# A gated recurrence of 256 steps on one core: steps written out, gate biases brought in by ScalarE, and the split state packed

## The reference

```python
ys = cond / 16
d = rsqrt(einsum('bi,io->bo', ys * ys, W * W) + 1e-8)
x = x + einsum('bsi,io->bso', x * ys[:, None, :], W) * d[:, None, :]

# H starts as cond; xz, xr, xh are x at this step times Wx*, plus bx*
Z = sigmoid(xz + H @ Whz.T + bhz)
R = sigmoid(xr + H @ Whr.T + bhr)
H_tilda = tanh(xh + (R * H) @ Whh.T + bhh)
H = Z * H + (1 - Z) * H_tilda
x[:, t] += H @ Whq.T + bhq
```

## Time and profile before

| | |
|---|---|
| device time, median of 3 runs | 682.16 us (681.14 to 682.66) |
| device time of the profiled execution | 683.9 us |
| its span, first to last instruction | 682.0 us |
| PE, PEld busy | 649.7 us (95%), 612.8 us (90%) |
| DVE, ACT, POOL busy | 456.9 us (67%), 201.5 us (30%), 16.2 us (2%) |
| mean granted TensorE clock | 0.529 of full speed |

### The profile page before, as it was taken

How to read it: one execution, slowest core, us unless ns; L and a number is a source line. 1 busy time by engine, 2 the same in 40 slices (tenths; PEclk the granted TensorE clock), 3 DMA queues, 4 the chain that set the end, 5 groups by cost and what they waited for, 6 DMA issues and landing times.

```text
span 682.0 us, 38427 instructions
## 1 busy us (share of the span) xinstructions
PE 649.7 (95%) x16076; PEld 612.8 (90%) x16076; DVE 456.9 (67%) x3690; ACT 201.5 (30%) x1543; POOL 16.2 (2%) x17
## 2 busy tenths in 40 slices
PE   4799999999969999999979999999996999999998
PEld 2399999999969999999978999999996999999997
DVE  3966676767647676766756667676764767676675
ACT  2033333333323333333332333333332333333332
POOL 2510000000000000000000000000000000000000
PEclk9965555555555555555555555555555555555555
DMA  7000000000000000000000000000000000000000
GB/s 258 0 11 5 3 12 3 12 4 12 4 7 12 4 11 5 3 12 4 11 7 11 5 3 12 3 12 4 12 4 7 12 4 11 5 3 12 4 11 11
DMA packets 7026, 9.32 MB, mean 14 GB/s; under 512 B 848, under 2 KB 5200, under 8 KB 6832
## 3 DMA queue, kind: packets, MB, share of 16 engines
q1 hardware_dynamic: 6288, 6.17, 2.7%
q10 hardware_dynamic: 544, 0.46, 0.2%
HBM read 4.40 MB, written 2.23 MB: 10 GB/s over the span
## 4 chain that ended last, share of the span: by engine, by line
PE 94%; issue 3%; DVE 2%; DMA 1%; SPq 0%; DVEq 0%; ACT 0%
PE chunk_bank L486 51%; PE z_rec_bank L486 16%; PE chunk_bank L446 12%; PE y_bank L452 6%; PE z_bank L446 6%; DMA x<-x_cm 1%; PE chunk_bank L459 1%; DVE xs L319 1%; PE r_bank L439 1%; PE chunk_bank L439 1%; PE y_bank L439 0%; DVE lin L329 0%; DVE bias_rows L360 0%; DVE r_hidden L402 0%; SPq L202 0%
## 5 line engine op out<-in xcount | busy, mean ns | idle before, releaser
L486 PEld LDWEIGHTS chunk_bank<-hidden,w_part 128*128 128x128 bf16 x6144 | 198.4, 106 | 27.5 <-issue 10.6
L486 PE MATMUL chunk_bank<-hidden,w_part 128*128 128x8 bf16 x6144 | 210.6, 173 | 9.6 <-issue 9.6
L486 PE MATMUL chunk_bank<-r_hidden,w_part 128*128 128x8 bf16 x6144 | 206.3, 169 | 0.3 <-DVE r_hidden L402 0.3
L486 PEld LDWEIGHTS chunk_bank<-r_hidden,w_part 128*128 128x128 bf16 x6144 | 184.6, 105 | 8.1 <-DVE r_hidden L402 0.4
L486 PE MATMUL z_rec_bank<-hidden,w_part 128*128 128x24 bf16 x3072 | 148.7, 201 | 6.9 <-issue 6.9
L425 DVE TENSOR_TENSOR_SCAN hidden<-scan_mul,hidden 128x24 f32<-128x24 f32 x512 | 80.8, 199 | 75.7 <-ACT hidden L281 70.3
L486 PEld LDWEIGHTS z_rec_bank<-hidden,w_part 128*128 128x128 bf16 x3072 | 123.7, 111 | 7.2 <-issue 7.2
L398 DVE TENSOR_TENSOR r_hidden<-r_bank,hidden 128x8 f32<-128x8 f32 x256 | 42.6, 166 | 127.7 <-ACT r_bank L275 127.7
L278 ACT ACTIVATE scan_mul<-z_pre 128x16 f32<-128x16 f32 x256 | 57.1, 223 | 203.8 <-DVE z_pre L410 203.8
L275 ACT ACTIVATE r_bank<-chunk_bank 128x8 f32<-128x8 f32 x256 | 41.5, 162 | 233.5 <-PE chunk_bank L486 233.5
L446 PE MATMUL chunk_bank<-x,w_in 128*128 (+1 forms) x272 | 101.4, 479 | 0.0
(11 more groups left out here) (48 smaller groups left out, 304.6 us busy)
## 6 DMA issues: line engine op xcount, KB each, us to landing
out_cm<-result SPq DMA_DIRECT2D x17, 128.0 KB, 2.1
x<-x_cm SPq DMA_DIRECT2D x4, 512.0 KB, 9.9
w_rec<-w_rec_cm SPq DMA_DIRECT2D x1, 768.0 KB, 8.8
w_in<-w_in_cm SPq DMA_DIRECT2D x1, 768.0 KB, 9.9
w_mod<-w_mod_cm ACTq DMA_DIRECT2D x1, 256.0 KB, 3.1
w_out<-w_out_cm SPq DMA_DIRECT2D x1, 256.0 KB, 9.6
bias_rows<-gate_bias ACTq DMA_DIRECT2D x1, 192.0 KB, 3.2
cond<-cond_cm SPq DMA_DIRECT2D x1, 8.0 KB, 2.7
```

What stands on the lines that cost most here:

```text
L486: return nc.tensor.matmul(cols, w_part[wp][:, gate, k, m * P:(m + 1) * P], moving, start=first, stop=True, skip_group_check=True)
```

## The change

The four loops are gone: every engine's 256 steps stand one after another, and waits compare with constants. `x1` holds the 16 real blocks alone, the first block has no output product and the last no input product (16 steps without bulk). The matmuls `in_bias` are gone: ahead of the recurrence TensorE sums the two bias rows into z_rec_bank (four matmuls of one column), VectorE copies the sums out, GpSimd spreads them over 128 columns (`bias_wide`), and ScalarE copies these into the chunk banks ahead of each block's input products (`seed_gate`, in j = 4 to 7). h is still scanned into `hidden`, but its three parts are now in `hidden_parts` without gaps; the first of them is made by one more VectorE copy (`h_packed`) behind the two subtractions, and gate Z and the output product read from there. The first groups of gate R read the scanned word as before. `take_z` moves to j = 8 and 9, and the even groups of the linear layer use the chunk banks of parity 0.

```diff
-        bias_rows = sb("bias_rows", [96, 2, C])
-        ones = sb("ones", [96, BC], bf16)
+        bias_rows = sb("bias_rows", [2, 2, C])
+        ones = sb("ones", [2, 1])
...
-        hidden = sb("hidden", [P, KC, SLOTS, PARTS * PART])
+        hidden = sb("hidden", [P, KC, SLOTS, 2 * PART])
+        hidden_parts = sb("hidden_parts", [P, KC, SLOTS, PARTS, B])
...
+        def h_scanned(k, slot):
+            return hidden[:, k, slot, 2:PART:3]
+        def h_scanned_high(k, slot):
+            return hidden_bf[:, k, slot, 5:2 * PART:6]
         def h_word(k, slot, part=0):
-            return hidden[:, k, slot, PART * part + 2:PART * (part + 1):3]
+            return hidden_parts[:, k, slot, part, :]
         def h_parts(k, slot, lo, hi):
-            return hidden_bf[:, k, slot, 2 * PART * lo + 5:2 * PART * hi:6]
+            return hidden_parts_bf[:, k, slot, 2 * B * lo + 1:2 * B * hi:2]
...
-        lin_bank = [[r_bank, y_bank], chunk_bank[1]]
+        lin_bank = chunk_bank
...
         def _(pool):
-            nc.gpsimd.memset(x1[:, :, 0:BC], 0.0)
-            nc.gpsimd.memset(hidden[:, :, BLOCK:SLOTS - 1, 2::3], 0.0)
-            nc.gpsimd.memset(x1[:, :, (1 + NB) * BC:], 0.0).then_inc(x1_ready, 1)
...
+            pool.wait_ge(bias_ready, 2)
+            for gate in range(2):
+                wide = nc.gpsimd.tensor_copy(bias_wide[:, :, gate, :],
+                                             gate_bias_cm[:, gate, :].unsqueeze(2).to_broadcast([P, KC, BC]))
+            wide.then_inc(wide_ready, 1)
             for i in range(GROUPS):
...
         def _(act):
...
-            act.dma_start(bias_rows[:, :, :], gate_bias).then_inc(ld_bias, 16)
+            act.dma_start(bias_rows[:, :, :], gate_bias[0:2, :, :]).then_inc(ld_bias, 16)
...
+            def seed_gate(parity, gate, k):
+                nc.scalar.activation(chunk_bank[parity][k][:, gate * BC:(gate + 1) * BC], bias_wide[:, k, gate, :],
+                                     ACT.Copy).then_inc(gates_seeded, 1)
+            act.wait_ge(wide_ready, 1)
+            act.wait_ge(lin_ready, 3)
+            for i in range(2 * KC):
+                seed_gate(0, i // KC, i % KC)
             act.wait_ge(z_seeded, 1)
-            with act.Fori(0, ITERS) as it:
-                for s in range(BODY):
+            for t in range(T):
...
+                if n + 1 < NB and j in (4, 5, 6, 7):
+                    if j == 4:
+                        act.wait_ge(lin_ready, GROUPS)
+                    seed_gate(1 - p, (j - 4) // KC, j % KC)
...
             def split_h(slot, t1):
                 for k in range(KC):
                     dve.wait_ge(h_ready[k], t1)
-                    nc.vector.tensor_tensor(h_word(k, slot, 1), h_word(k, slot), h_parts(k, slot, 0, 1), ALU.subtract
+                    nc.vector.tensor_tensor(h_word(k, slot, 1), h_scanned(k, slot), h_scanned_high(k, slot), ALU.subtract
                                             ).then_inc(h_rest[k], 1)
...
-                nc.vector.tensor_copy(hidden[:, :, slot, 4:4 + PART:3], h_word(every_chunk, slot))
+                nc.vector.tensor_copy(h_word(every_chunk, slot), h_scanned(every_chunk, slot)).then_inc(h_packed, 1)
+                nc.vector.tensor_copy(hidden[:, :, slot, 4:4 + PART:3], h_scanned(every_chunk, slot))
...
-            nc.vector.memset(ones[:, :], 1.0)
+            nc.vector.memset(ones[:, :], 1.0).then_inc(bias_ready, 1)
...
-            dve.wait_ge(ld_bias, 16)
-            for group in (64, 32):
-                rows = bias_rows[group:group + 32, :, :]
-                own(nc.vector.tensor_tensor(rows, rows, high(rows), ALU.subtract))
             modulate(1)
             scale_x(3)
-            rows = bias_rows[64:96, :, :]
-            nc.vector.tensor_tensor(rows, rows, high(rows), ALU.subtract).then_inc(bias_ready, 1)
+            dve.wait_ge(bias_summed, 1)
+            nc.vector.tensor_copy(gate_bias_cm[:, :, :], z_rec_bank[:, KC * B:KC * B + 2 * KC]
+                                  .rearrange("p (g k) -> p g k", g=2)).then_inc(bias_ready, 1)
...
         def _(pe):
...
-            def in_bias(parity, gate, m, steps):
-                return nc.tensor.matmul(pre(parity, gate, m, steps.start, steps.stop),
-                                        high(bias_rows[:, :, :])[:, gate // 2, m * P:(m + 1) * P],
-                                        ones[:, 0:(steps.stop - steps.start) * B], start=False, stop=True,
-                                        skip_group_check=True)
...
+            def bulk(n, j):
...
+                if j < 4:
+                    if n > 0:
...
+                elif n + 1 < NB:
+                    if j == 8:
+                        pe.wait_ge(gates_seeded, 2 * KC * (n + 2))
                     if j == 4:
-                        pe.wait_ge(x1_ready, 1 + GROUPS)
+                        pe.wait_ge(x1_ready, 1 + (n + 1) * GROUPS // NB)
...
+            pe.wait_ge(ld_bias, 16)
+            pe.wait_ge(bias_ready, 1)
+            for gate in range(2):
+                for k in range(KC):
+                    at = KC * B + gate * KC + k
+                    mm = nc.tensor.matmul(z_rec_bank[:, at:at + 1], bias_rows[:, gate, k * P:(k + 1) * P], ones[:, :],
+                                          start=False, stop=True, skip_group_check=True)
+            mm.then_inc(bias_summed, 1)
...
-            pe.wait_ge(x1_ready, 2)
+            pe.wait_ge(x1_ready, 1)
             for gate in (Z, R, G):
                 if gate == R:
-                    pe.wait_ge(bias_ready, 1)
+                    pe.wait_ge(gates_seeded, 2 * KC)
...
-            with pe.Fori(0, ITERS) as it:
-                for s in range(BODY):
+            for t in range(T):
...
                 pe.wait_ge(z_seeded, t + 1)
+                pe.wait_ge(h_packed, t + 1)
...
-                    if j in BIAS_AT:
-                        in_bias(1 - p, *BIAS_AT[j])
-            for k in range(KC):
-                pe.wait_ge(h_ready[k], T + 1)
-            pe.wait_ge(res_ready, KC * NB)
+            pe.wait_ge(h_packed, T + 1)
+            pe.wait_ge(res_ready, KC * (NB - 1))
```

More of the change, by code:

```diff
@@ L215, in _ @@
                     sp.dma_start(w_in[:, :, :, :], w_in_cm).then_inc(ld_win, 16)
-            def store(n, parity):
+            for n in range(NB):
                 sp.wait_ge(res_ready, (n + 1) * KC)
[L220 to L228, removed]
+                sp.dma_start(out[:, :, (n + 1) * BC:(n + 2) * BC], result[:, n % 2, :, :]).then_inc(stored[n % 2], 16)
+            for q in range(2):
+                sp.wait_ge(stored[q], 16 + 16 * (NB // 2))
         @block.gpsimd
@@ L430, in _ @@
-            dve.wait_ge(y_ready, NB + 1)
+                    out=result[:, n % 2, k, :], in0=y_bank[:, k * BC:(k + 1) * BC], scalar=bq[:, k:k + 1],
+                    in1=x1[:, k, n * BC:(n + 1) * BC], op0=ALU.add, op1=ALU.add).then_inc(res_ready, 1)
+            for t in range(T):
+                p, j, n = t // BLOCK % 2, t % BLOCK, t // BLOCK
+                before = (t - 1) % SLOTS
+                for k in range(KC):
+                    dve.wait_ge(r_ready[k], t + 1)
+                    nc.vector.tensor_tensor(r_hidden[:, k, 0, :], r_gate[k], h_scanned(k, before),
+                                            ALU.mult).then_inc(rh_ready[k], 1)
+                for k in range(KC):
+                    dve.wait_ge(rh_ready[k], t + 1)
+                    nc.vector.tensor_tensor(r_hidden[:, k, 1, :], r_hidden[:, k, 0, :], rh_parts(k, 0, 1),
+                                            ALU.subtract).then_inc(rh_rest[k], 1)
+                for k in range(KC):
+                    dve.wait_ge(rh_rest[k], t + 1)
+                    nc.vector.tensor_tensor(r_hidden[:, k, 2, :], r_hidden[:, k, 1, :], rh_parts(k, 1, 2),
+                                            ALU.subtract).then_inc(rh_rest2[k], 1)
+                dve.wait_ge(rec_z, t + 1)
+                nc.vector.tensor_reduce(
+                    z_pre[:, :, :], z_rec_bank[:, 0:KC * Z_GROUPS * B].rearrange(
+                        "p (m g b) -> p m b g", m=KC, g=Z_GROUPS),
+                    axis=mybir.AxisListType.X, op=ALU.add).then_inc(pre_z, 1)
+                if n > 0 and j in (4, 5):
+                    finish(n - 1, j - 4)
+                if n + 1 < NB and j in (8, 9):
+                    if j == 8:
+                        dve.wait_ge(z_ready, n + 1)
+                    take_z(1 - p, j - 8)
+                for k in range(KC):
+                    dve.wait_ge(g_ready[k], t + 2)
+                    nc.vector.tensor_tensor_scan(hidden[:, k, t % SLOTS, 0:PART], scan_mul[:, k, :],
+                                                 hidden[:, k, before, 2:2 + PART], 0.0, ALU.mult, ALU.add
+                                                 ).then_inc(h_ready[k], 1)
+                split_h(t % SLOTS, t + 2)
@@ L443, in in_tile @@
             def in_tile(n, parity, gate, m, k):
-                first = k == 0 and (gate == R or (gate == Z and m == 0))
```

(3 more changed lines are left out.)

136 lines of the change are left out of this document (45 added, 91 removed).

## The result

The changed kernel takes 657.99 us (median of 4 runs, 656.98 to 658.91) against 682.08 us of the kernel before: a ratio of 0.9648, with a 95% interval from 0.9627 to 0.9668. The forecast was 656.2. The profiled execution took 658.91 us with a span of 657.0, where 657.9 us was forecast for it.

A forecast was written before the change was run, and what follows sets the result against it. The prediction took each step's chain of waits through gate R, R * h, gate G, tanh and scan as the bound. Terms -17.3 - 7.4 - 0.8 - 1.0 + 0.5 = -26.0 took 682.16 to 656.2 us; range 645 to 665.

The forecast's parts named there:

- The loops go: At the three loop turns, writing the steps out removes a stall of 5.77 us each: -17.3 us.
- The bias matmuls go: In steps j = 8 to 15, removing them saves 0.46 us in each of 16 blocks: -7.4 us.
- Sixteen steps lose their bulk: In the sixteen steps without an fp32 input matmul, each gains 0.05 us: -0.8 us.
- ScalarE's seeds: Sixty ScalarE copies of 128 columns in j = 4 to 7 fall in its idle time: cost 0.
- The packing copy: VectorE's new copy ahead of gate Z's matmuls has 0.08 us to spare at Z's wait: cost 0.
- Rival 2: At gate Z's new wait, the packing copy lands 0.33 us late: slower, 702 us; chance 3%.
- Z's packed columns: Gate Z's matmuls may speed up from 35 to 28 ns, but G waits for R * h: 0.
- The clock (rival 3): TensorE's granted clock returns to 0.99 if the stalls hold it down: 10 us more gained, 646 us; chance 5%.
- Ahead of the recurrence: In the start before the first step, bias sums and spreading against less loading and fewer matmuls: -1.0 us, bounds -2.5 and +2.
- The end: The last output product waits for the packing copy instead of the scan: +0.5 us.
- the ring: Each step's chain of waits: gate R, sigmoid, R * h, gate G, tanh, scan; other TensorE matmuls only fill its two gaps.

The follow-up runs named there:

- the run with late copies: The changed kernel with four more VectorE copies to a spare tile in each step, ahead of the packing copy: 687.0 us, ratio 1.007 to the kernel before.
- the spread: The changed kernel with ScalarE spreading the biases from the four sums, without GpSimd's two copies: 656.07 us, ratio 0.9614 to the kernel before.
- the held-back additions: The changed kernel with GpSimd's last four additions held back until step 60: 659.72 us, ratio 0.9668 to the kernel before.
- unpacked kernel: The changed kernel with h's parts again at a stride of three words, without the packing copy and its wait: 658.98 us, ratio 0.9656 to the kernel before.

## Why the prediction was right, step by step

- **The loops go, -17.3.** Right: 17.4 us with that edit alone, 11.4 for two of three turns. The term used the kernel's own turns; the run without bias matmuls shows that another program would have had others.
- **The bias matmuls go, -7.4.** Right in mechanism, 6.9 by the steps. Their duration of 0.26 us each would have given 33 us. What bound the steps after them was the scan, as the step said: gate R's first matmul stood 0.15 us behind the end of the scan of chunk 0 in the steps that follow a bias matmul, and stands 0.07 behind it in all steps with a bulk now.
- **Sixteen steps lose their bulk, -0.8.** Right in mechanism, 16 x 0.036 = 0.6 in size: they take 2.371 against 2.407, with R's first matmul 0.06 behind the scan.
- **ScalarE's seeds, 0.** Right. ScalarE's idle time ahead of the sigmoid of R is 0.89 us, and still 0.70 in j = 5 to 8, which follow a seed.
- **The packing copy, 0.** Right in the result and wrong in its margin: 0.02 us to spare at Z's wait and not 0.08, since the second wait is an instruction of 0.05 us. Rival 2 had named just that and its place; the run with late copies showed its price, and that the kernel ends up slower than before if the copy lands 0.32 us late. With a slack of 0.02 and not 0.08 the term of 0 was a narrow thing.
- **Z's packed columns, 0.** Right: Z's pitch fell from 35 to 27 ns and G didn't move.
- **The clock (rival 3).** Did not come back. Over the stretch from 60 to 190 us TensorE was busy 129.23 of 130 us at a granted clock of 0.50, as in the earlier trace rows, with all stalls gone. Gaps of TensorE were not what held it at the lower level.
- **Ahead of the recurrence, -1.0.** The term that failed, in size and in sign: the start to step 1 grew by 0.7 us instead (38.71 against 38.02). Up to TensorE's first input product the gain was there, 29.79 instead of 31.32, though the bias sums took 1.8 us and not 0.9 (each fp32 matmul is two) and GpSimd's copies 1.1 each and not 0.8. What the term left out lies behind that product: from it to the sigmoid of step 1 it is 8.92 us now and was 6.70. The table load moved onto the path with the steps written out. And GpSimd's additions, pushed back by its copies, reached further into step 0 and held VectorE: with GpSimd out of the way the same stretch takes 7.2 us in the runs with the spread and with the held-back additions, so 1.7 of the 2.2 us go with it. It is the one that decides when step 1 begins, and its sign was in the trace of the kernel before, where the first two subtractions of step 0 take 0.77 us together. That 190 KB less to load give 0.4 us can't be told from these runs: VectorE's first scaling started at 7.6 to 8.5 us in the five traces of the changed start and at 7.6 to 9.2 in the four of the start before.
- **The end, +0.5.** Right: 7.55 against 7.10, and 7.09 in the run without the packing copy and its wait.

The total agrees better than the terms do, and part of that is luck. The 254 steps from step 1 on gave 26.1 us, of which the loops are 17.3, the bias matmuls 6.9 and the steps without bulk 0.6. Some 1.3 us are left, and 1.2 of them are the ordinary steps, 2.412 us before and 2.407 after (0.005 x 240), for which the sum has no term; they make up for most of the 1.7 us by which the start missed its forecast. A step of the unpacked kernel took 2.412 us too; since 2.400 was seen in another set of runs, what sets this difference isn't settled. The medians of the unpacked and the changed kernel don't tell them apart.

## What to carry to other kernels

In a recurrence, ask of each engine what its first instruction of a group waits for, and cost an edit by the gap in the ring it lies in: two edits that shortened TensorE's busy time by similar amounts (33 us for the bias matmuls, and 27 for Z's packed columns, whose matmuls were busy 148.7 us before and 121.5 after) were worth 7 us and nothing. Moving work to an idle engine ahead of a loop can cost later: look at when that engine's queue then ends, and whether operations of an engine on the path last longer beside it. When a loop is written out, look again at what used to stand ahead of it, such as a table load.

## What the runs showed of the hardware

- The way back of the hardware loop cost 5.5, 5.8 and 6.7 us on average in three programs that differ in the body alone.
- Bf16 matmuls of 24 columns followed each other every 35 ns with columns twelve bytes apart and every 27 ns with four, at a granted clock of 0.50. With 8 columns it was 27 at either stride.
- A second semaphore on a weight load came as an instruction of 0.05 us: 0.14 us from the end of the copy to the first matmul.
- VectorE operations of 0.17 us with their inputs in SBUF lasted up to 1.3 us beside a GpSimd addition of 512 columns, and ended with it; one lasted 3.29 us, until the last of three additions had ended.
- TensorE was busy for 129.23 of 130 us, and for 298.21 of 300 from 300 us on, at a granted clock of 0.50 throughout.
- With the loop, the sigmoid's table was loaded once ahead of the first step's wait and once in each of the three turns; with the steps written out, it is loaded once, behind the wait for gate R's first product, with its 1.28 us on the path.
